# First attention, last two head pairs: the reciprocal of the denominators by exp(-ln) on ScalarE and a Newton step on VectorE

## The chip, the cores and the metric

The kernel runs on one core of one Trainium2 chip. The metric is the device time of one execution in microseconds (us), the median of the runs shown. A core has five engines that take their instructions in order and meet through semaphores: TensorE (PE, matrix products), VectorE (DVE), ScalarE (ACT, activations by function tables), GpSimd (POOL) and SyncE (SP, which issues most transfers here).

## The reference, cut to what matters

Two layers of a graph network with attention and feed-forward parts on 1250 tokens of width 1024. The change lies in the first layer's linear attention, 16 heads of 64 columns, which the kernel takes as 8 pairs of heads:

```
q = elu(xn @ Wq.T + bq) + 1
k = elu(xn @ Wk.T + bk) + 1
v = xn @ Wv.T + bv
KV = einsum('bhsd,bhsm->bhmd', k, v)
Z = 1 / (einsum('bhsd,bhd->bhs', q, k.sum(axis=2)) + 1e-06)
attn = einsum('bhsd,bhmd,bhs->bshm', q, KV, Z)
out = attn @ Wo.T + bo
```

Z is what the change computes in another way. The second layer's attention has no denominator.

## The kernel before, in words

Everything runs in single precision with each operand split into a high and a low part. The program is a row of phases: embedding, `attention` (tag m0), `project_and_count` (tag o), the graph layer (gl), routing and experts, and the same attention function again for layer two (tag m), its projection and the last feed-forward part. At the end of a phase all engines meet at a barrier (`Phase.__exit__`, L103), so the next phase begins when the slowest engine has arrived.

`attention` goes over j = 0 to 3, two head pairs at a time. A pair is called q here: 0 to 7, with A = 6 and B = 7 the last two. Tokens lie in three tiles t of 512, 496 and 242 columns. For each j TensorE computes keys and values in ten chunks (`keys`, L1632 to L1638), gathers the memory KV with the sum of the keys (`gather`, L1651), computes queries (`query`, L1613 to L1619) and then the numerator and the denominator of each tile (`attend`, L1668 to L1670), each in a PSUM bank of its own. `softly` is True in the first attention alone.

What follows `attend` is the stretch that the change touches. On ScalarE `den(q, t)` (L1751) waits for `at_done`, and for the `at_out` of the tile two before it, since `dn` has two slots; it copies the denominator plus 1e-6 into SBUF and raises `den_raw`. On VectorE `evict(q, t)` waits for `den_raw`, takes the reciprocal in place (L1869), drains, waits until the store of the pair before has left `ats`, multiplies it with the numerator (L1876) and raises `at_out`. SyncE then stores the tile (`store`, L1552), and TensorE may write the two banks again. The slots `dn` and `ats` lie in `xr`, of which 512 columns, 2560 to 3071, are unused.

The order on each engine is written out by hand. After the last keys it is, on ScalarE: `out_hi(0)`, `ask(B, 0)`, `memory`, `out_hi(1)`, `ask(B, 1)`, `out_hi(2)`, `out_hi(3)`, `den(A, 0)`, `ask_high(B, 0)`, `den(A, 1)`, `ask_high(B, 1)`, `ask(B, 2)`, `pairs_high`, `ask_high(B, 2)`, `one_high(A)`, `den(B, 0)`, `den(A, 2)`, `one_high(B)`, `den(B, 1)`, `den(B, 2)`. `ask` makes relu (L1732, L1733) and exp (L1736) of a query tile, `ask_high` (L1743) its high part, `out_hi` (L173) the high part of an output weight, `pairs_high` (L1780) that of the first token block of pairs 0 to 5, `one_high` (L1784) that of one more pair. On VectorE: `out_lo(0)`, `answer(B, 0)`, `memory` and `memory_low`, `out_lo(1)`, `answer(B, 1)`, `out_lo(2)`, `out_lo(3)`, `evict(A, 0)`, `ask_low(B, 0)`, `evict(A, 1)`, `ask_low(B, 1)`, `answer(B, 2)`, `pairs_low`, `ask_low(B, 2)`, `one_low(A)`, `evict(B, 0)`, `evict(A, 2)`, `one_low(B)`, `evict(B, 1)`, `evict(B, 2)`. On TensorE: `attend(A, 0)`, `attend(A, 1)`, `query(B, 2)`, `attend(A, 2)`, `attend(B, 0)`, `begin_out(0)`, `begin_out(1)`, `attend(B, 1)`, `begin_out(2)`, `begin_out(3)`, `attend(B, 2)`, and then 16 products that nobody reads (`fill`, L219), which follow `at_out[A, 2]`. `begin_out` (L365) is the first part of the next phase's product and waits for `pairs_low`.

ScalarE evaluates Exp, Ln, Sqrt, Tanh and Silu from tables. The loads of these tables (ACT_TABLE_LOAD) are no lines of the kernel's text: the compiler puts them into ScalarE's stream, and the trace gives each the line of the activation that it serves.

Of the kernel before, what the change touches and what calls it, by code (L numbers as in the profile page):

```python
# [10 lines left out]
ALU = mybir.AluOpType  # L11
ACT = mybir.ActivationFunctionType
AX = mybir.AxisListType

P = 128
N = 1250
E = 20000
D = 1024
# [204 lines left out]
def tile(t):  # L223
    return slice(CUTS[t], CUTS[t + 1])


def width(t):
    return CUTS[t + 1] - CUTS[t]


def flat(ap):
    return ap.rearrange("p a b -> p (a b)")
# [1234 lines left out]
def attention(nc, rest, tag, xh, xl, at, w_dram, bq_dram, bkv_dram, softly, raw, first, then, xr, xr_free, kept, ps, begun, place, onto, slots_free, freed, settled, beside=None, taken=(), room=None):  # L1467
# [5 lines left out]
    with Phase(nc, tag) as p:  # L1473
# [33 lines left out]
        qh, ql = p.sb("qh", [P, TM], F32R), p.sb("ql", [P, TM], F32R)  # L1507
        ks, mf = p.sb("ks", [P, 2]), own("mf", [P, 2, W2])
        mh, ml = p.sb("mh", [P, 2, W2], F32R), p.sb("ml", [P, 2, W2], F32R)
        spare = flat(xr)  # L1510
        ats, dn = spare[:, 0:TM], [spare[:, D + 512 * b:D + 512 * b + 512] for b in (1, 2)]
        bank = [ps[:, b] for b in range(8)]
        q_bank = lambda q, t: bank[3 - tile_nth[q, t] % 2][:, 0:width(t)]
# [12 lines left out]
        def num_den(q, t):  # L1526
            if t == 2:
                b = bank[0 if q % 2 == 0 else 1 if q == B else 7]
                return b[:, 0:width(t)], b[:, width(t):2 * width(t)]
            n, d = ((7, 6), (4 if softly else 6, 5))[t]  # L1530
            return bank[n][:, 0:width(t)], bank[d][:, 0:width(t)]
# [54 lines left out]
        @block.gpsimd  # L1586
        def _(e):
            e.wait_ge(*settled.last())
            for a in range(2):
                for b in range(2):  # L1590
                    i = e.memset(mask[64 * a:64 * a + 64, 64 * b:64 * b + 64], 1.0 if a == b else 0.0)
                i.then_inc(consts.sem)
                e.wait_ge(*consts["mask", a])
            for t in () if softly else xr_free[-1:]:
                e.wait_ge(*t.last())
            e.memset(mf[:], 0.0)
            e.memset(kv[:, 0, :, :, W2:KW].bitcast(F32), 1.0)
            e.memset(kv[:, 1, :, :, W2:KW].bitcast(F32), 0.0).then_inc(consts.sem)
            if beside:
                beside(e, p)  # L1600
# [113 lines left out]
        @block.scalar  # L1714
        def _(e):
            def hi(u):
                e.wait_ge(*arrived(u))
                if u[1] == Q:
                    e.wait_ge(*q_done[u[0] - 1, 2])
                elif u[0] >= 2:  # L1720
                    e.wait_ge(*kv_done[u[0] // 2 - 1, TC - 1])
                else:
                    e.wait_ge(*slots_free[kv_slot(u)])
                e.activation(held(0, u), raw[:, nth[u] % SLOTS], ACT.Copy).then_inc(high.sem)

            def ask(q, t):
                b, o, f, n = bq[:, q:q + 1], q_bank(q, t), qf[:, tile(t)], qn[:, tile(t)]
                e.wait_ge(*(q_done[q, t] if q or t else begun["q"]))
                if q:
                    e.wait_ge(*q_low[q - 1, t])  # L1730
                if softly:
                    e.activation(n, o, ACT.Relu, bias=nbq[:, q:q + 1], scale=-1.0)  # L1732
                e.activation(f, o, ACT.Relu, bias=b).then_inc(q_raw.sem)  # L1733
                e.drain()
                if softly:
                    e.activation(n, n, ACT.Exp, scale=-1.0).then_inc(q_exp.sem)  # L1736

            def ask_high(q, t):
                if softly:
                    e.wait_ge(*q_map[q, t])  # L1740
                if q:
                    e.wait_ge(*at_done[q - 1, t])
                e.activation(qh[:, tile(t)], qf[:, tile(t)], ACT.Copy).then_inc(q_high.sem)  # L1743

            def den(q, t):
                if softly:
                    n = out_nth[q, t]
                    e.wait_ge(*at_done[q, t])
                    if n >= 2:
                        e.wait_ge(*at_out[outs[n - 2]])  # L1750
                    e.activation(dn[n % 2][:, 0:width(t)], num_den(q, t)[1], ACT.Copy, bias=1e-6).then_inc(den_raw.sem)  # L1751

            def key(j, c):
                n, r = chunk_nth[j, c], rows_of(c)
                s = n % RING
                f = kvf[0:r, s].rearrange("p (q n) -> p q n", q=2)
                e.wait_ge(*kv_raw[j, c])
                if softly:
                    g = neg[0:r, s].rearrange("p (q n) -> p q n", q=2)
                    e.activation(g, f[:, :, 0:P], ACT.Relu, scale=-1.0)  # L1760
                    e.drain()
                    e.activation(g, g, ACT.Exp, scale=-1.0).then_inc(kv_exp.sem)
                    e.wait_ge(*kv_map[j, c])
                if n >= RING:
                    e.wait_ge(*m_used[chunks[n - RING]])
                e.activation(kv[0:r, 0, s, :, 0:W2], f, ACT.Copy).then_inc(kv_high.sem)  # L1766

            def memory(j):
                e.wait_ge(*m_raw[j])
                e.activation(mh[:, :, 0:MW], mf[:, :, 0:MW], ACT.Copy).then_inc(m_high.sem)  # L1770

            def out_hi(s):
                e.wait_ge(*ahead.loaded[s][s])
                e.wait_ge(*kv_done[J[-1], TC - 1])
                out.make_hi(e, s).then_inc(o_high.sem)

            def pairs_high():
                e.wait_ge(*pairs_in["pairs"])
                e.wait_ge(*q_done[B, 2])
                e.activation(oh[:, part], ar[:, part], ACT.Copy).then_inc(at_high.sem)  # L1780

            def one_high(q):
                e.wait_ge(*at_out[q, 0])
                e.activation(oh[:, q], ats[:, 0:P], ACT.Copy).then_inc(at_high.sem)  # L1784

            hi((0, K))
            hi((0, V))
            e.wait_ge(*ld["bq"])
            e.activation(nbq[:], bq[:], ACT.Copy, scale=-1.0)
            e.drain()  # L1790
            hi((1, K))
            hi((1, V))
            for t in xr_free if softly else ():
                e.wait_ge(*t.last())
            for j in J:
                a, b = 2 * j, 2 * j + 1
                if j == 0:
                    for t in T:
                        ask(a, t)
                    for t in T:  # L1800
                        ask_high(a, t)
                    hi((b, Q))
                else:
                    ask(a, 0)
                    hi((b, V))
                    den(a - 1, 0)
                    ask_high(a, 0)
                    ask(a, 1)
                    den(a - 1, 1)
                    ask_high(a, 1)  # L1810
                    hi((b, Q))
                    ask(a, 2)
                    den(a - 1, 2)
                    ask_high(a, 2)
                for c in C:
                    key(j, c)
                if j < J[-1]:
                    hi((a + 2, K))
                    ask(b, 0)
                    memory(j)  # L1820
                    hi((a + 2, V))
                    ask(b, 1)
                    hi((b + 2, K))
                    hi((a + 2, Q))
                    ask(b, 2)
                    for t in T:
                        den(a, t)
                        ask_high(b, t)
            out_hi(0)
            ask(B, 0)  # L1830
            memory(J[-1])
            out_hi(1)
            ask(B, 1)
            out_hi(2)
            out_hi(3)
            den(A, 0)
            ask_high(B, 0)
            den(A, 1)
            ask_high(B, 1)
            ask(B, 2)  # L1840
            pairs_high()
            ask_high(B, 2)
            one_high(A)
            den(B, 0)
            den(A, 2)
            one_high(B)
            den(B, 1)
            den(B, 2)

        @block.vector  # L1850
        def _(e):
# [12 lines left out]

            def evict(q, t):
                o, i = num_den(q, t)[0], dn[out_nth[q, t] % 2][:, 0:width(t)]
                if softly:
                    e.wait_ge(*den_raw[q, t])
                    e.reciprocal(i, i)  # L1869
                    e.drain()  # L1870
                else:
                    e.wait_ge(*at_done[q, t])
                if q:
                    e.wait_ge(*stored[t][q - 1])
                if softly:
                    e.tensor_tensor(ats[:, tile(t)], o, i, ALU.mult).then_inc(at_out.sem)  # L1876
                else:
                    e.tensor_copy(ats[:, tile(t)], o).then_inc(at_out.sem)
# [1535 lines left out]
```

## Time and profile before

| | us |
|---|---|
| median of 3 runs | 2318.83 |
| lowest, highest | 2316.47, 2319.75 |
| the profiled execution, its own time | 2314.61 |
| its span in the trace | 2312.9 |
| PE busy in it | 2226.0 (96%) |
| DVE busy | 1512.6 (65%) |
| ACT busy | 1015.3 (44%) |
| mean granted TensorE clock | 0.98 of full |

The span is the stretch from the first to the last instruction of the profiled execution; 1.7 us of its own time lie outside it. All start times in the rows are us from the span's start. "Busy" of an engine is the sum of its instructions' time; the granted clock is given as a share of full speed. The first attention runs from about 119 to 516.8 us of the span, and the last two pairs' `evict` from 490.9 to 514.3 us.

### The profile page before, as it was taken

Reading aid. Unit: us, or ns where it says so; the run is one execution under the profiler, and the core shown is the slowest. Engines: PE = TensorE matmul, PEld = TensorE weight load, DVE = VectorE, ACT = ScalarE, POOL = GpSimd, SP = SyncE. Lnnn points to the kernel's source line nnn. Section 1 sums busy time; section 2 is a strip of 40 time slices with the busy share of each in tenths; the row PEclk is TensorE's granted clock in tenths of the full one; section 3 lists DMA queues with packets and bytes.
Section 4 is the critical chain, followed back from the end, with each engine's and each line's share of the span. In section 5 each row is a group of like instructions: output and inputs, shape, how many; then the busy total and the mean of one; then the engine's idle time right before and its main releaser. Section 6 shows DMA issues by size and latency. Waiting matters only on the chain. (4 is left out here: it accounts for less than half of the span.)

```text
span 2312.9 us, 29634 instructions
## 1 busy us (share of the span) xinstructions
PE 2226.0 (96%) x10816; PEld 1820.2 (79%) x10816; DVE 1512.6 (65%) x2245; ACT 1015.3 (44%) x1515; POOL 253.9 (11%) x256
## 2 busy tenths in 40 slices
PE   7999999988989999989999999999999999999998
PEld 5788888867868888876888888867888888878886
DVE  8746374568869888866999999957743233345422
ACT  4134243338735545426888888851122122121220
POOL 0077773000010000030000000001000000000000
PEclk9999999999999999969999999999999999999999
DMA  5431231124448635164554555136421120134314
GB/s 191 160 99 41 50 79 29 62 73 142 146 170 318 238 133 220 63 255 141 192 199 177 208 178 188 65 103 214 135 86 35 48 82 31 59 106 153 121 46 150
DMA packets 114122, 299.91 MB, mean 130 GB/s; under 512 B 18802, under 2 KB 42218, under 8 KB 113974
## 3 DMA queue, kind: packets, MB, share of 16 engines
q1 hardware_dynamic: 103094, 276.52, 34.4%
q0 software_dynamic: 10880, 21.48, 3.3%
q8 instruction: 86, 1.41, 0.3%
q14 instruction: 62, 0.51, 0.1%
HBM read 295.24 MB, written 124.16 MB: 181 GB/s over the span
## 5 line engine op out<-in xcount | busy, mean ns | idle before, releaser
L2793 DVE TENSOR_TENSOR ex_wl<-exlast,ex_wh 128x1024 fp32r<-128x1024 f32 x216 | 252.9, 1220 | 9.1 <-ACT ex_wh L2862 8.6
L2862 ACT ACTIVATE ex_wh<-exlast 128x1024 fp32r<-128x1024 f32 x216 | 218.1, 1059 | 17.3 <-PE ex_pu L2816 8.5
L1322 POOL DMA_INDIRECT scratch_slots<-packed x160 | 197.4, 1234 | 57.4 <-issue 57.4
L365 PE MATMUL ps<-kept,xh 128*128 128x512 f32 (+2 forms) x480 | 159.2, 418 | 3.4 <-DVE xl L689 1.8
L1632 PE MATMUL ps<-kept,xl 128*128 128x512 f32 (+1 forms) x640 | 159.3, 391 | 0.0
L1634 PE MATMUL ps<-kept,xh 128*128 128x512 f32 (+1 forms) x640 | 158.4, 390 | 0.0
L1638 PE MATMUL ps<-kept,xh 128*128 128x512 f32 (+1 forms) x640 | 158.3, 390 | 0.0
L2192 PE MATMUL gl_bank<-gl_gh,gl_al 125*128 125x512 f32 x385 | 151.0, 392 | 3.1 <-DVE gl_al L2407 3.0
L2193 PE MATMUL gl_bank<-gl_gl,gl_ah 125*128 125x512 f32 x385 | 150.2, 390 | 0.0
L2194 PE MATMUL gl_bank<-gl_gh,gl_ah 125*128 125x512 f32 x385 | 150.0, 390 | 0.0
L1634 PEld LDWEIGHTS ps<-kept,xh 128*128 128x128 f32 (+1 forms) x640 | 118.6, 185 | 26.8
L1638 PEld LDWEIGHTS ps<-kept,xh 128*128 128x128 f32 (+1 forms) x640 | 118.6, 185 | 26.7
L2793 DVE TENSOR_TENSOR ex_wl<-exfirst,ex_wh 128x1024 fp32r<-128x1024 f32 x108 | 127.3, 1221 | 11.1 <-ACT ex_wh L2862 11.1
L1632 PEld LDWEIGHTS ps<-kept,xl 128*128 128x128 f32 (+1 forms) x640 | 114.4, 186 | 22.1
L2862 ACT ACTIVATE ex_wh<-exfirst 128x1024 fp32r<-128x1024 f32 x108 | 111.0, 1056 | 31.2 <-DMA exfirst<-in_experts 16.0
L1766 ACT ACTIVATE m_kv<-m_kvf 128x512 fp32r<-128x512 f32 (+1 forms) x40 | 25.3, 632 | 205.5 <-DVE m_kvf L1898 205.5
L1890 DVE TENSOR_TENSOR m_kvf<-ps,m_bkv 128x512 f32<-128x512 f32 (+1 forms) x40 | 27.7, 692 | 131.1 <-PE ps L1638 131.1
L365 PEld LDWEIGHTS ps<-kept,xh 128*128 128x128 f32 (+2 forms) x480 | 91.0, 190 | 25.6 <-DVE xl L689 2.0
L2250 ACT ACTIVATE gl_ah<-gl_thaf 125x625 fp32r<-125x625 f32 x80 | 58.2, 728 | 82.7 <-DVE gl_thaf L2397 82.7
L2816 PE MATMUL ex_pg<-ex_wl,ex_xh 128*128 128x512 f32 x216 | 89.4, 414 | 0.6 <-DVE ex_xl L2901 0.6
L2192 PEld LDWEIGHTS gl_bank<-gl_gh,gl_al 125*128 125x128 f32 x385 | 72.3, 188 | 20.3 <-DVE gl_al L2407 4.4
L2397 DVE TENSOR_TENSOR gl_thaf<-gl_thaf,counts 125x625 f32<-125x625 f32 x80 | 64.2, 807 | 33.0 <-ACT gl_thaf L2237 31.5
(530 smaller groups left out, 4968.8 us busy)
## 6 DMA issues: line engine op xcount, KB each, us to landing
exlast<-in_experts SPq DMA_DIRECT2D x216, 512.0 KB
exfirst<-in_experts SPq DMA_DIRECT2D x112, 512.0 KB
scratch_seats<-raw SPq DMA_DIRECT2D x95, 512.0 KB
raw<-in_qkv SPq DMA_DIRECT2D x48, 512.0 KB, 4.9
xr<-scratch_res SPq DMA_DIRECT2D x27, 512.0 KB, 4.1
xr<-scratch_seats SPq DMA_DIRECT2D x27, 512.0 KB
scratch_res<-xr SPq DMA_DIRECT2D x25, 512.0 KB, 3.6
raw<-in_wo SPq DMA_DIRECT2D x16, 512.0 KB, 5.4
```

The costliest lines, as they stand in the source:

```text
L365: i = e.matmul(o, a, b[:, cut], start=first and n == 0, stop=final and n == 2)
L1322: e.indirect_dma_start(dram["slot_rows"], bass.IndirectOffsetOnAxis(idx[:, k:k + 1].bitcast(U32), 0), pay[:, k, :], None).then_inc(scat.se ...
L1632: e.matmul(o, xl[:, k, tokens(c)], cut(wh, k), start=k == 0, stop=False)
L1634: e.matmul(o, xh[:, k, tokens(c)], cut(wh, k), start=False, stop=False)
L1638: m = e.matmul(o, xh[:, k, tokens(c)], cut(wl, k), start=False, stop=k == KC - 1)
L2192: e.matmul(o, al[0:r, b, d], gh[0:r, c], start=c == 0, stop=False)
L2193: e.matmul(o, ah[0:r, b, d], gl[0:r, c], start=False, stop=False)
L2194: m = e.matmul(o, ah[0:r, b, d], gh[0:r, c], start=False, stop=c == TC - 1)
L2397: e.tensor_tensor(af[0:r, (s + 2 * h) % 4, 0:HWID[h]], th[0:r, b, 0:HWID[h]], cnt[0:r, s, cols(h)], ALU.mult).then_inc(a_raw.sem)
L2793: return e.tensor_tensor(wl[:, n % RING], raw[unit[1]], wh[:, n % RING].bitcast(F32), ALU.subtract)
L2816: m = e.matmul(o[:], a[:, i % 2, k], w[:, n, cut], start=k == 0 and w is wl, stop=k == KC - 1 and a is xh and w is wh)
L2862: e.activation(wh[:, n % RING], raw[unit[1]], ACT.Copy).then_inc(high.sem)
```

## The change

Pairs 0 to 5 stay as they are. For pairs A and B, six tiles, `den` computes exp(-ln(d + 1e-6)) on ScalarE instead of a copy. `evict` takes that value i as a first approximation of the reciprocal, computes z = (d + 1e-6) * i, y = -o * i and (z - 2) * y on VectorE (one Newton step, with o the numerator), each a scalar_tensor_tensor with a drain between them. A column `eps` of 1e-6 is set by GpSimd for the bias of Ln, and one Ln of one column stands on ScalarE ahead of `out_hi(0)`. `z` lies in the unused part of `xr`.

```diff
@@ attention
+        eps = own("eps", [P, 2]) if softly else None
         spare = flat(xr)
+        near = spare[:, 2 * D + 512:3 * D]
@@ gpsimd
             e.memset(mf[:], 0.0)
+            if softly:
+                e.memset(eps[:], 1e-6)
@@ scalar, den
-                    e.activation(dn[n % 2][:, 0:width(t)], num_den(q, t)[1], ACT.Copy, bias=1e-6).then_inc(den_raw.sem)
+                    d, i = num_den(q, t)[1], dn[n % 2][:, 0:width(t)]
+                    if q < A:
+                        e.activation(i, d, ACT.Copy, bias=1e-6).then_inc(den_raw.sem)
+                    else:
+                        e.activation(i, d, ACT.Ln, bias=eps[:, 0:1])
+                        e.drain()
+                        e.activation(i, i, ACT.Exp, scale=-1.0).then_inc(den_raw.sem)
@@ scalar
+            if softly:
+                e.activation(eps[:, 1:2], eps[:, 0:1], ACT.Ln)
             out_hi(0)
             ask(B, 0)
@@ vector, evict
+                z, y = near[:, 0:width(t)], ats[:, tile(t)]
                 if softly:
                     e.wait_ge(*den_raw[q, t])
-                    e.reciprocal(i, i)
+                    if q < A:
+                        e.reciprocal(i, i)
+                    else:
+                        e.drain()
+                        e.scalar_tensor_tensor(z, num_den(q, t)[1], 1e-6, i, ALU.add, ALU.mult)
                     e.drain()
...
-                if softly:
+                if softly and q >= A:
+                    e.scalar_tensor_tensor(y, o, -1.0, i, ALU.mult, ALU.mult)
+                    e.drain()
+                    e.scalar_tensor_tensor(y, z, -2.0, y, ALU.add, ALU.mult).then_inc(at_out.sem)
+                elif softly:
                     e.tensor_tensor(ats[:, tile(t)], o, i, ALU.mult).then_inc(at_out.sem)
```

## Rows read from the trace of the kernel before

**Rows 1.** Busy time by stretch: us, PE, PEld, DVE, ACT, POOL, clock, DMA share, GB/s.

```profile
492.00:495.70 3.70, 0.03 (x1) 0.03 (x1) 3.63 (x4) 1.35 (x3) 0.00 (x0) 0.96 0.66 216
495.70:501.30 5.60, 2.90 (x6) 1.79 (x6) 5.53 (x6) 0.84 (x3) 0.00 (x0) 0.72 0.24 92
501.30:506.00 4.70, 4.66 (x13) 3.70 (x14) 4.53 (x5) 0.51 (x2) 0.00 (x0) 0.64 0.00 0
506.00:510.60 4.60, 4.60 (x24) 3.85 (x22) 4.52 (x5) 0.90 (x2) 0.00 (x0) 1.00 0.23 84
514.30:516.80 2.50, 0.00 (x0) 0.00 (x1) 0.00 (x0) 0.00 (x0) 0.00 (x0) 1.00 0.16 50
```

**Rows 2.** VectorE in order of time, end of the first attention: start, us, instruction.

```profile
490.89 3.35 DVE L1869 RECIPROCAL xr<-xr 128x512 f32<-128x512 f32 x1
494.31 0.69 DVE L1876 TENSOR_TENSOR xr<-ps,xr 128x512 f32<-128x512 f32 x1
...
500.34 0.95 DVE L1926 TENSOR_TENSOR ox<-ar,ox 128x768 fp32r<-128x768 f32 x1
...
512.11 1.66 DVE L1869 RECIPROCAL xr<-xr 128x242 f32<-128x242 f32 x1
513.84 0.41 DVE L1876 TENSOR_TENSOR xr<-ps,xr 128x242 f32<-128x242 f32 x1
```

**Rows 3.** TensorE in order of time, the same stretch; in brackets its idle time before.

```profile
501.34 4.61 PE L365 MATMUL ps<-kept,ox 128*128 128x512 f32 x12 [2.74 <-DVE ox L1926]
...
507.15 2.93 PE L365 MATMUL ps<-kept,ox 128*128 128x512 f32 x12
...
510.61 3.63 PE L219 MATMUL ps<-rest 128*128 128x512 bf16 x16
516.83 2.10 PE L219 MATMUL ps<-rest 128*128 128x512 bf16 x9 [2.59 <-PEq L103]
```

**Rows 4.** ScalarE in order of time, the same stretch.

```profile
480.28 0.68 ACT L1733 ACTIVATE counts<-ps,m_bq 128x512 f32<-128x512 f32 x1
481.04 0.63 ACT L1736 ACTIVATE counts<-counts 128x512 f32<-128x512 f32 x1
...
487.54 1.99 ACT L173 ACTIVATE kept<-raw 128x1024 fp32r<-128x1024 f32 x2
489.43 0.58 ACT L1751 ACTIVATE xr<-ps 128x512 f32<-128x512 f32 x1
...
500.45 0.41 ACT L1743 ACTIVATE m_qh<-counts 128x242 fp32r<-128x242 f32 x1 [7.02 <-DVE counts L1859]
...
506.06 0.31 ACT L1784 ACTIVATE ox<-xr 128x128 fp32r<-128x128 f32 x1 [4.25 <-DVE xr L1876]
```

**Rows 5.** ScalarE in order of time, the first Exp of this attention, with its table load.

```profile
128.26 0.68 ACT L1733 ACTIVATE counts<-ps,m_bq 128x512 f32<-128x512 f32 x1
129.00 1.28 ACT L1736 ACT_TABLE_LOAD   x1
130.30 0.63 ACT L1736 ACTIVATE counts<-counts 128x512 f32<-128x512 f32 x1
```

**Rows 6.** ScalarE's groups by line: table loads, count, busy, mean ns.

```profile
L302 ACT ACT_TABLE_LOAD x2 | 2.6, 1283 | 0.8 <-PEq L3406 0.8
L1736 ACT ACT_TABLE_LOAD x1 | 1.3, 1283 | 0.1
...
L3241 ACT ACT_TABLE_LOAD x1 | 1.3, 1283 | 0.0
```

**Rows 7.** Groups by line and shape, 200 to 515 us: busy, mean ns.

```profile
L1869 DVE RECIPROCAL xr<-xr 128x512 f32<-128x512 f32 x8 | 26.8, 3347 | 0.1
L1869 DVE RECIPROCAL xr<-xr 128x496 f32<-128x496 f32 x8 | 26.0, 3247 | 0.0
L1869 DVE RECIPROCAL xr<-xr 128x242 f32<-128x242 f32 x8 | 13.3, 1658 | 0.0
L1876 DVE TENSOR_TENSOR xr<-ps,xr 128x496 f32<-128x496 f32 x8 | 5.4, 675 | 0.6
L1894 DVE SCALAR_TENSOR_TENSOR counts<-counts 128x256 f32<-128x256 f32 x27 | 11.6, 430 | 26.2 <-ACT counts L1762 26.2
L1733 ACT ACTIVATE counts<-ps,m_bq 128x242 f32<-128x242 f32 x7 | 3.2, 454 | 0.0
```

**Rows 8.** GpSimd in order of time, start of the first attention.

```profile
120.19 0.11 POOL L1597 MEMSET m_kv<- 128x12 f32 x1
```

## The prediction

> **What bounds the kernel now.** I read the busy time by stretch first, then the engines in order of time in the last 25 us of the first attention, then the groups by shape for prices. The chain that ended last says nothing here, since it goes back only to the second half of the program. Before the wall VectorE has next to no gap: 5.53 of 5.60 us, 4.53 of 4.70, 4.52 of 4.60 [rows 1]. Its first reciprocal of these two pairs starts at 490.89 and its last instruction ends at 514.25 (513.84 + 0.41) [rows 2]. TensorE waits for it: 2.74 us for pairs_low (L1926), and its fill products end at 510.61 + 3.63 = 514.24 [rows 3]. So two engines reach the barrier together, and the next phase starts 2.6 us later, at 516.8 [rows 1, 3]. ScalarE has room: it waits 7.02 and 4.25 us for VectorE [rows 4]. What this stretch gains or loses passes whole into the time only if the later engine of the two moves, and ScalarE's room is finite.
>
> **What VectorE sheds.** Six reciprocals, two of each shape, go: 2 x (3.35 + 3.25 + 1.66) = 16.5 us [rows 7]. Each tile gets three scalar_tensor_tensor instead of one product. Of such an operation the rows have only 256 columns, 0.43 us; a two-operand product takes 0.69 for 512, 0.675 for 496 and 0.41 for 242 [rows 2, 7]. I take 0.69, 0.67 and 0.41; the low end is the product's price, the high end 2 x 0.43 = 0.86 for 512. After a drained instruction the next one starts 0.07 us later (490.89 + 3.35 = 494.24 against 494.31) [rows 2]. An evict of 512 goes from 3.35 + 0.07 + 0.69 = 4.11 to 3 x 0.69 + 2 x 0.07 = 2.21, one of 496 from 3.99 to 2.15, one of 242 from 2.14 to 1.37: 9.0 us less over six tiles, if i is ready in time.
>
> **What ScalarE takes on, without loads.** A Copy of 0.58 [rows 4] becomes Ln and Exp. Ln reads PSUM with a bias column as L1733 does, 0.68; Exp reads SBUF as L1736 does, 0.63; between them lie 0.08 (480.96 to 481.04) [rows 4]. That is 1.39 for 512, an estimated 1.36 for 496, and 0.454 + 0.08 + 0.41 = 0.94 for 242, with 0.41 from L1743, which reads SBUF too [rows 4, 7]. With 7.02 and 4.25 us of waiting [rows 4] this alone would be hidden.
>
> **The table loads.** Here the sum is decided. A switch of function costs a load of 1.28 us: it starts 0.06 after the activation before it has ended (128.94, 129.00), and the activation starts 0.02 after it (130.28, 130.30) [rows 5]. In drained order Exp starts at +1.36 instead of +0.08, so a load costs 1.28; in undrained order it also costs the overlap of about 0.1 that neighbours have, 1.4. The trace has nine loads: L302 twice, and one each at L1736, L2214, L2215, L2528, L2884, L3056 and L3241 [rows 6]. The tabled functions in order are Sqrt, Exp, Sqrt, Tanh, Sqrt, Exp, Silu, Sqrt, Silu: nine runs of one function and nine loads. No change of function came free, and none was served by a set fetched for an earlier function. No row shows Ln, so its load is bounded by zero (Ln and Exp under one load) and by one load at every change. I take every change, the pattern of all nine [rows 6]. Then the added single Ln loads one set, ask(B, 0)'s Exp the other, and each of the six dens loads twice: 14 loads, 18 us of ScalarE.
>
> [...]
>
> **The sum in order of time.** The single Ln and its load end before 477.6; out_hi(0) moves by 1.5, under VectorE's wait for answer(B, 0) and without price. The load ahead of ask(B, 0)'s Exp moves answer(B, 0), memory and what follows on ScalarE by 1.28: out_hi(3) ends at 490.8 instead of 489.5 (487.54 + 1.99) [rows 4]. From there, starts overlapped as now:
> den(A, 0) takes 1.28 + 0.02 + 0.68 + 0.06 + 1.28 + 0.02 + 0.63 = 3.97 and ends at 494.8. VectorE, free at about 492.3 (out_lo(3) is late by 1.3 too), waits 2.5; evict(A, 0) ends at 497.05 instead of 495.0 (494.31 + 0.69) [rows 2].
> ask_high(B, 0), then den(A, 1) of 3.9, end at 499.3; evict(A, 1) ends at 501.5, and ask_low(B, 1), answer(B, 2) and pairs_low follow until 503.2, where they now end at 501.29 (500.34 + 0.95) [rows 2]: 1.9 later. TensorE's begin_out and all behind it move by 1.9, its fill ends at 516.2.
> ScalarE gets answer(B, 2) at 502.4, does ask_high(B, 2) and one_high(A) until 503.0, den(B, 0) until 507.0, den(A, 2) of 3.5 until 510.5, one_high(B), den(B, 1) until 514.7, den(B, 2) until 518.25. Nothing but these loads holds it now: the waits for at_done are over before each. VectorE's evict(B, 2) of 1.37 ends at 519.65 instead of 514.25.
> That is **+5.4 us** at the barrier, with ScalarE as the new bound. The 16.5 us of reciprocals are all given back as VectorE's waits for den_raw. The low end: one load fewer in the chain, +4. The high end: three operations at 0.86 on the last tiles, and a colder TensorE after the wall (below), +8.
>
> **The rest.** GpSimd's memset of two columns is like L1597, 0.11 us [rows 8], 11 us ahead of the first Exp at 130.30 [rows 5] and before its queue of scatters, which it moves by that 0.1 at most: nothing. No transfer is added. The six stores follow at_out, so the last ones go out 5.4 later; the projection reads them behind the barrier that moves with them. The waits of SyncE have nothing else queued behind them. The z slot is unused space. The drain ahead of z comes after a wait, on an empty engine. TensorE's pause at the wall grows from 2.59 [rows 3] to about 6 us (516.2 to 522.2). The clock was granted at 0.72 and 0.64 after pauses of 3.7 and 2.74 us, where twelve products of 512 took 4.61 instead of 2.93 us [rows 1, 3]. [...]
>
> **Own time and median.** The sum is made against the profiled execution, 2314.61 us, span 2312.9. That is 4.2 us (0.18%) under the median of 2318.83. The difference is set on the median: 2318.83 + 5.4 = 2324.2. What a measurement of this kernel can tell from no change is about 0.2%, 4.6 us; the forecast lies just beyond it.
>
> **Rival 1: one set serves both (not slower).** Ln and Exp stay under one table load, that of the added single Ln, which falls into slack. Then den(A, 0) ends at 489.43 + 1.39 = 490.8, as VectorE comes free at 490.9; evict(A, 0) ends 1.85 earlier, evict(A, 1) 3.7, and pairs_low at 497.6 instead of 501.3. TensorE's row of begin_out, attend, begin_out, attend and fill follows without a gap and ends at 514.24 - 3.65 = 510.6, VectorE at 509.4. So TensorE's fill sets the wall and the gain is 3.65 us, not 9: 2315.2, or 2313.5 if the shorter pauses keep the clock up and begin_out takes 2.93 instead of 4.61 [rows 1, 3]. It decides if no load stands in den. For it: the single Ln is placed where only a set that serves both would make sense of it. Against: the nine loads at nine changes [rows 6].
> [...] No row shows Ln under any load. Chance 0.13.
>
> **Rival 2: a load costs more in the pipeline.** If a load between two activations also empties the pipe for over a microsecond, as no row shows but the drained order might bring, all 13 loads in the chain grow: at 1 us each 13 us more, +18, 2337. Against it: 0.06 and 0.02 [rows 5]. Chance 0.04.
>
> **Rival 3: the loads come, but less of them counts.** Some lie in waits that I took as over, such as den(B, 1)'s and den(B, 2)'s for TensorE, or VectorE's operations are dearer while ScalarE is late anyway and hide. The wall then moves by under 4.6 us, most likely +3: 2321.8. It is the lower part of my forecast's own spread. Chance 0.25, against 0.58 for the forecast proper.
>
> **How the numbers follow.** Forecast and rivals 2 and 3 give slower or slightly slower. The range has to hold the forecast's +4 to +8, rival 3 and the scatter of medians (2316.5 to 2319.8 for one kernel); it leaves out most of rivals 1 and 2: 2317.5 to 2329.5. Faster by over 0.2%: rival 1 with the clock held, 0.05. Slower by over 0.2%: the forecast and rival 2, 0.62. Within: rival 3 and the rest of rival 1, 0.33.
>
> **What would show it.** Right: 23 table loads instead of 9, two in each den; no reciprocal after 490; VectorE waiting for ACT at L1751's successor before each z, about 2 us at a time; the fill ending about 3 us before VectorE; the next phase starting near 522. Wrong: one or two more loads only (rival 1: TensorE's fill last, next phase near 513); a gap of about a microsecond beside each load (rival 2); loads with ScalarE waiting between them (rival 3); scalar_tensor_tensor of 512 far from 0.69 us.

## The result and the profile after

The change makes the kernel slightly slower: 2322.57 us median of 11 runs (2319.52 to 2325.31) against 2318.76 of 11 runs before (2316.47 to 2320.0), ratio 1.0016, 95% interval 1.0009 to 1.0024, so 3.8 us (2.1 to 5.6). That lies in the stated range and in the forecast's direction, but inside the 0.2% that the prediction called no change.

First ScalarE's groups by line, table loads only. The six single loads in the phases behind are there as before [rows 6], so there are 23 loads instead of 9.

```profile
L1759 ACT ACT_TABLE_LOAD x6 | 7.7, 1283 | 0.1
L1761 ACT ACT_TABLE_LOAD x6 | 7.7, 1283 | 0.3
L302 ACT ACT_TABLE_LOAD x2 | 2.6, 1283 | 0.8 <-PEq L3429 0.8
L1740 ACT ACT_TABLE_LOAD x2 | 2.6, 1283 | 0.1
L1840 ACT ACT_TABLE_LOAD x1 | 1.3, 1283 | 0.0
```

L1759 is Ln in den, L1761 its Exp, L1840 the single Ln, L1740 the Exp in ask. Each den loads twice, and the Exp of ask(B, 0), which had its table, loads again behind the single Ln. ScalarE in order of time, the last pairs of the changed kernel (beside [rows 4, 5] of before):

```profile
476.94 0.63 ACT L1776 ACTIVATE m_kv<-counts 98x512 fp32r<-98x512 f32 x1 [0.49 <-DVE counts L1917]
477.59 1.28 ACT L1840 ACT_TABLE_LOAD   x1
...
481.25 0.69 ACT L1736 ACTIVATE counts<-ps,m_nbq 128x512 f32<-128x512 f32 x1 [1.21 <-PE ps L1623]
...
482.58 1.28 ACT L1740 ACT_TABLE_LOAD   x1
...
490.37 2.00 ACT L173 ACTIVATE kept<-raw 128x1024 fp32r<-128x1024 f32 x2
492.39 1.28 ACT L1759 ACT_TABLE_LOAD   x1
493.68 0.69 ACT L1759 ACTIVATE xr<-ps,counts 128x512 f32<-128x512 f32 x1
494.43 1.28 ACT L1761 ACT_TABLE_LOAD   x1
495.72 0.63 ACT L1761 ACTIVATE xr<-xr 128x512 f32<-128x512 f32 x1
...
504.04 0.41 ACT L1747 ACTIVATE m_qh<-counts 128x242 fp32r<-128x242 f32 x1 [0.79 <-DVE counts L1871]
...
518.13 1.28 ACT L1761 ACT_TABLE_LOAD   x1
519.42 0.41 ACT L1761 ACTIVATE xr<-xr 128x242 f32<-128x242 f32 x1
```

From 492.39 to 519.83 ScalarE has one wait, 0.79 us. Its two longest waits before were 7.02 and 4.25 us [rows 4]. VectorE in order of time, first and last evict (beside [rows 2]):

```profile
496.45 0.69 DVE L1886 SCALAR_TENSOR_TENSOR xr<-ps,xr 128x512 f32<-128x512 f32 x1 [2.64 <-ACT xr L1761]
497.22 0.69 DVE L1895 SCALAR_TENSOR_TENSOR xr<-ps,xr 128x512 f32<-128x512 f32 x1
497.98 0.69 DVE L1897 SCALAR_TENSOR_TENSOR xr<-xr 128x512 f32<-128x512 f32 x1
...
503.92 0.95 DVE L1949 TENSOR_TENSOR ox<-ar,ox 128x768 fp32r<-128x768 f32 x1
...
519.93 0.41 DVE L1886 SCALAR_TENSOR_TENSOR xr<-ps,xr 128x242 f32<-128x242 f32 x1 [1.35 <-ACT xr L1761]
...
520.90 0.41 DVE L1897 SCALAR_TENSOR_TENSOR xr<-xr 128x242 f32<-128x242 f32 x1
```

VectorE now waits for ScalarE's Exp before each of the six evicts, 1.30 to 3.32 us at a time, 12.8 us in all. TensorE in order of time (beside [rows 3]):

```profile
504.93 5.49 PE L365 MATMUL ps<-kept,ox 128*128 128x512 f32 x12 [2.65 <-DVE ox L1949]
...
515.27 3.63 PE L219 MATMUL ps<-rest 128*128 128x512 bf16 x16
523.98 4.00 PE L219 MATMUL ps<-rest 128*128 128x512 bf16 x9 [5.08 <-PEq L103]
```

TensorE's fill ends at 518.90, 2.4 us before VectorE at 521.31. So ScalarE's chain, through VectorE, alone sets the barrier.

To compare profiles I use **the stretch**: from the start of the last high part of keys and values (m_kv, the first line of ScalarE above) to the first transfer issued in the projection. All profiles, in us; "ahead" runs to the first relu of the attention, "pairs 0 to 5" from there to the stretch, "projection" from the stretch's end to the first table load of the graph layer, "rest" to the end of the span. begin_out is the first group of 12 products in the stretch.

| kernel | added loads | ahead | pairs 0 to 5 | stretch | begin_out | projection | rest |
|---|---|---|---|---|---|---|---|
| before | 0 | 127.7 | 347.7 | 41.41 | 4.61 | 158.0 | 1638.1 |
| before2 | 0 | 130.7 | 347.8 | 41.40 | 4.33 | 159.1 | 1638.8 |
| changed | 14 | 129.3 | 347.6 | 47.01 | 5.49 | 158.8 | 1638.2 |
| again | 14 | 129.3 | 347.7 | 47.00 | 5.36 | 158.4 | 1638.8 |
| fill26 | 14 | 130.6 | 347.6 | 46.99 | 5.29 | 158.0 | 1639.9 |
| recip_kept | 14 | 129.6 | 347.7 | 50.75 | 4.60 | 158.9 | 1637.6 |
| nowarm | 12 | 130.8 | 347.7 | 45.71 | 5.49 | 158.8 | 1642.2 |
| paired | 10 | 129.5 | 347.7 | 45.30 | 5.08 | 158.3 | 1638.4 |
| oneset | 1 | 129.2 | 347.7 | 36.04 | 3.06 | 158.2 | 1638.1 |
| oneset2 | 1 | 128.7 | 347.9 | 36.00 | 3.03 | 158.2 | 1639.3 |
| oneset_fill8 | 1 | 130.3 | 347.6 | 36.86 | 4.41 | 158.0 | 1636.1 |
| oneset_all | 0 | 131.2 | 344.7 | 37.60 | 4.21 | 158.6 | 1638.5 |
| copied | 0 | 129.3 | 347.6 | 36.00 | 3.03 | 158.2 | 1640.8 |

Ratios below are against runs of the kernel before taken beside the others: medians 2320.38 us for again, oneset, copied and nowarm, 2317.51 for fill26, recip_kept, oneset_fill8 and oneset_all, 2316.75 for paired. Outside oneset_all, which changes more than the stretch, the difference of two such medians comes out between 3.1 us under and 0.8 us over what the stretch shows. So the medians give the direction, and the stretch the size.

### The profile page after: what moved, and what is told of

The parts are those of the page before. It is cut to its first block and busy times, and to the rows that moved or that the text cites. A ratio compares the mean times of both kernels' runs of the same rounds, so it can differ in the third digit from the quotient of the medians.

```text
span 2320.9 us, 29680 instructions
## 1 busy us (share of the span) xinstructions
PE 2233.4 (96%) x10816; PEld 1825.3 (79%) x10816; DVE 1503.5 (65%) x2251; ACT 1037.4 (45%) x1536; POOL 253.1 (11%) x257
## 5 line engine op out<-in xcount | busy, mean ns | idle before, releaser
L1638 PE MATMUL ps<-kept,xh 128*128 128x512 f32 (+1 forms) x640 | 158.3, 389 | 0.0
L1642 PE MATMUL ps<-kept,xh 128*128 128x512 f32 (+1 forms) x640 | 158.2, 389 | 0.0
```

The lines of the kernel that those rows point to most:

```text
L1638: e.matmul(o, xh[:, k, tokens(c)], cut(wh, k), start=False, stop=False)
L1642: m = e.matmul(o, xh[:, k, tokens(c)], cut(wl, k), start=False, stop=k == KC - 1)
```

## The experiments

**again** and **before2**, both kernels unedited.

> The changed kernel once more, unedited. 'The stretch' is here and below the time from the start of the last high part of keys and values in the first attention (98 rows, ScalarE) to the first transfer issued in the projection; it is 516.79 - 475.38 = 41.4 us before and 523.95 - 476.94 = 47.0 us after. If the 5.6 us are the change's, this profile has 46.9 to 47.1 again and the time is 3.8 to 5.6 us above before's. If they were scatter of one execution, the stretch comes out elsewhere between 41 and 47.

> The kernel before, unedited, for a second profile. Theory (what lies outside the stretch is scatter): the stretch is 41.4 us again, and the part ahead of it, which reached the last high part of keys and values at 475.4 us in the first profile and at 476.9 to 478.4 in those of the changed kernels, comes out within 475 to 479. Rival (the change costs 1.5 us ahead of the stretch): 475.4 again.

again: 2322.93 us, ratio 1.0016 (1.0007 to 1.0025), stretch 47.00. The medians differ by 2.6 us, or 3.7 by the ratio, just under the 3.8 to 5.6 expected. before2, a single run: 2319.46 us, stretch 41.40. ScalarE and SyncE in before2, the two lines that bound its stretch, and between them the last instructions of TensorE and VectorE:

```profile
478.51 0.63 ACT L1766 ACTIVATE m_kv<-counts 98x512 fp32r<-98x512 f32 x1 [0.49 <-DVE counts L1894]
...
513.43 3.63 PE L219 MATMUL ps<-rest 128*128 128x512 bf16 x16
...
516.96 0.41 DVE L1876 TENSOR_TENSOR xr<-ps,xr 128x242 f32<-128x242 f32 x1
...
519.91 0.32 SPq L1094 DMA_DIRECT2D o_slots<-scratch_slots  x1
```

The stretch repeats within 0.01 us in either kernel, so the 5.6 us are the change's. What lies ahead varies by 3 us between two profiles of one and the same kernel, and the changed kernel's later arrival lies within that. Here TensorE's fill ended at 517.06, 0.31 us before VectorE at 517.37, and the stretch was the same: it is VectorE, 2.54 us ahead of the next phase in both profiles of before, that sets the barrier there.

**oneset**: a table set, number 6 in the edit, is loaded by hand ahead of the single Ln; that it serves both Ln and Exp is shown by this run's rows.

```diff
             if softly:
+                e.add_instruction(mybir.InstLoadActFuncSet(name=nc.get_next_instruction_name(), act_func_set_id=6))
                 e.activation(eps[:, 1:2], eps[:, 0:1], ACT.Ln)
```

> One edit to the changed kernel: the table set that holds both Ln and Exp is loaded by hand ahead of the single Ln, so that no further load is needed in the attention (1 added load instead of 14). Theory (ScalarE's loads are the bound): VectorE's evicts start as ScalarE's Exp ends, TensorE's fill becomes last, and the stretch is 41.4 - 3.65 = 37.8 us; the time is 3.7 us below before's, 7 to 9 below the changed kernel's. Rival (VectorE's three operations with drains, or the clock, cost what the change lost): the stretch stays above 43 us.

2312.01 us, ratio 0.997 (0.996 to 0.998), stretch 36.04. That is 11 us off the changed kernel's stretch and 5.4 off before's. The trace has 10 table loads instead of 23: the nine of before and the one by hand (L1840), of 1.28 us. None stands in a den or ahead of ask(B, 0)'s Exp (L1740): in each den Exp starts 0.06 to 0.07 us after Ln has ended (491.62, 491.68), with no load between them. ScalarE, then TensorE, then VectorE of oneset in order of time:

```profile
477.54 1.28 ACT L1840 ACT_TABLE_LOAD   x1
478.83 0.20 ACT L1841 ACTIVATE counts<-counts 128x1 f32<-128x1 f32 x1
...
482.55 0.63 ACT L1740 ACTIVATE counts<-counts 128x512 f32<-128x512 f32 x1
...
490.95 0.67 ACT L1759 ACTIVATE xr<-ps,counts 128x512 f32<-128x512 f32 x1
491.68 0.63 ACT L1761 ACTIVATE xr<-xr 128x512 f32<-128x512 f32 x1
...
503.95 0.67 ACT L1759 ACTIVATE xr<-ps,counts 128x496 f32<-128x496 f32 x1 [0.78 <-PE ps L1674]
```

```profile
495.51 0.47 PE L1672 MATMUL ps<-m_ql,m_mh 128*128 128x512 f32 x1 [1.94 <-DVE m_ql L1876]
...
499.51 3.06 PE L365 MATMUL ps<-kept,ox 128*128 128x512 f32 x12 [2.37 <-DVE ox L1950]
...
507.17 3.63 PE L219 MATMUL ps<-rest 128*128 128x512 bf16 x16
```

```profile
492.58 0.69 DVE L1887 SCALAR_TENSOR_TENSOR xr<-ps,xr 128x512 f32<-128x512 f32 x1
...
509.37 0.41 DVE L1898 SCALAR_TENSOR_TENSOR xr<-xr 128x242 f32<-128x242 f32 x1
```

Exp needs no load there, ScalarE waits for TensorE again (0.78 us), VectorE ends at 509.78 and TensorE's fill at 510.80: the fill is last, as rival 1 had it. The expected 37.8 took begin_out at 4.61; it took 3.06, which is nearly all of the difference of 1.8 (the parts are in the account of rival 1 below). With and without 13 of the loads, the same Ln, Exp and three operations differ by 11 us, so the rival that blames VectorE's operations falls.

**copied**: it leaves out Ln and Exp, the single Ln too, so its output is not the attention's.

```diff
-                        e.activation(i, d, ACT.Ln, bias=eps[:, 0:1])
-                        e.drain()
-                        e.activation(i, i, ACT.Exp, scale=-1.0).then_inc(den_raw.sem)
+                        e.activation(i, d, ACT.Copy, bias=1e-6, scale=1e-9).then_inc(den_raw.sem)
```

> Leaves out Ln and Exp: for the last two pairs ScalarE makes one scaled copy, as long as the copy before; VectorE does the three operations of the Newton step on it. Theory: no loads, ScalarE has room again, so the stretch is as with the one set, 37.8 us or up to 0.7 less (Ln and Exp gone from between TensorE's last product and evict), bounded by TensorE's fill. Rival (VectorE's chain bounds it once the loads are gone): the stretch is over 0.5 us shorter than with the one set, and VectorE's last instruction ends after the fill.

2315.57 us, ratio 0.998 (0.9971 to 0.9989), stretch 36.00, the same as with the one set to 0.04 us. Ln and Exp themselves cost nothing on the path; the loads do. VectorE ends at 509.18, the fill at 510.76. Its median lies 3.6 us above oneset's at the same stretch; the part called rest has 2.7 us of that in the profiles, and why stays open.

**nowarm**: the line `e.activation(eps[:, 1:2], eps[:, 0:1], ACT.Ln)` is taken out.

> One edit to the changed kernel: the single Ln ahead of out_hi(0) is left out, so its load and the load ahead of ask(B, 0)'s Exp go (12 added loads instead of 14). Theory (loads count one for one where ScalarE has no slack behind them): the load ahead of the single Ln was hidden, the one at ask(B, 0) was not, so the stretch is 1.3 us shorter, 45.7. Rival (loads this early are hidden anyway): 47.0 as before the edit.

2323.51 us, ratio 1.0015 (1.0005 to 1.0025), stretch 45.71, 1.3 less, the value expected for one load on the path and one in slack. The load of the single Ln is the one in slack: behind it, in the changed kernel, ScalarE still waits 1.21 us for TensorE before ask(B, 0). The medians cannot tell 1.3 us; the stretch can.

**paired**: the first four dens in two groups.

```diff
-            den(A, 0)
+            dens((A, 0), (A, 1))
             ask_high(B, 0)
-            den(A, 1)
             ask_high(B, 1)
...
-            den(B, 0)
-            den(A, 2)
+            dens((B, 0), (A, 2))
```

with `dens` doing Ln of both, one drain, Exp of both.

> The changed kernel with its dens in two groups: Ln of (A, 0) and (A, 1), then Exp of both; Ln of (B, 0) and (A, 2), then Exp of both. No set is chosen by hand; 10 added loads instead of 14. Theory (ScalarE's stream, loads included, is the bound until its waits for others come back): evict(A, 1) starts 1.1 us earlier, pairs_low and begin_out too, den(B, 1) then waits for TensorE's attend(B, 1), and the stretch is 45.4 us (45.0 to 45.9), not 47.0. Rival (loads count one for one): 47.0 - 4 x 1.3 = 41.8.

2321.43 us, ratio 1.0019 (1.0009 to 1.0029), stretch 45.30, 1.7 less for four loads. ScalarE of paired in order of time:

```profile
503.30 0.41 ACT L1747 ACTIVATE m_qh<-counts 128x242 fp32r<-128x242 f32 x1 [2.68 <-DVE counts L1882]
...
503.92 1.28 ACT L1770 ACT_TABLE_LOAD   x1
505.22 1.04 ACT L1770 ACTIVATE xr<-ps,counts 128x512 f32<-128x512 f32 x2
506.31 1.28 ACT L1774 ACT_TABLE_LOAD   x1
507.61 0.92 ACT L1774 ACTIVATE xr<-xr 128x512 f32<-128x512 f32 x2
510.60 0.31 ACT L1807 ACTIVATE ox<-xr 128x128 fp32r<-128x128 f32 x1 [2.07 <-DVE xr L1908]
```

With fewer loads it waits again, 2.68 us instead of 0.79 for answer(B, 2) and 2.07 for evict(B, 0), so loads do not count one for one once the waits return. The size is as expected, but the second wait is for VectorE, not for TensorE's attend(B, 1).

**recip_kept**: the exp/ln part alone, with `ACT.Exp` of +ln and VectorE's old reciprocal and product for pairs A and B.

> The changed kernel without the Newton step: Ln and Exp with all their loads stay on ScalarE, with exp(+ln), and VectorE takes the reciprocal of it and one product, as before the change. Theory (ScalarE's loads bound the stretch, VectorE's saving lies in their shade): the stretch grows by much less than the 9.0 us that VectorE has more to do. evict(A, 1) and so answer(B, 2), for which ScalarE waits, come 2.1 to 3.7 us later, and the last evict takes 2.1 instead of 1.4: 49.5 to 51.4 us. Rival (VectorE's operations bound it): 47 + 9 = 56.

2325.08 us, ratio 1.0031 (1.0018 to 1.0043), stretch 50.75. VectorE has 9.0 us more to do than in the changed kernel (the prediction's sum) and the stretch grows by 3.7. VectorE, then ScalarE:

```profile
496.70 3.35 DVE L1882 RECIPROCAL xr<-xr 128x512 f32<-128x512 f32 x1 [2.56 <-ACT xr L1761]
500.12 0.69 DVE L1895 TENSOR_TENSOR xr<-ps,xr 128x512 f32<-128x512 f32 x1
```

```profile
506.26 0.41 ACT L1747 ACTIVATE m_qh<-counts 128x242 fp32r<-128x242 f32 x1 [2.70 <-DVE counts L1871]
```

So the two halves of the change stand apart. Ln and Exp with their loads cost 9.3 us (41.41 to 50.75), and on that chain the Newton step is worth 3.7 (50.75 to 47.0). Without loads it is worth 5.4 (41.4 to 36.0, copied).

**fill26**: `fill(e, bank[0], rest, 26 if softly else 6)`.

> One edit to the changed kernel: 26 products in TensorE's fill instead of 16, which nobody reads. They end at 515.3 + 26 x 0.227 = 521.2, as VectorE's last evict does (521.3), so the stretch stays 47.0. Theory (the long pause at the barrier lets TensorE's clock drop, which costs at the start of the projection): the pause is 2.6 to 2.8 instead of 5.1 us, the nine products after it take 2.1 instead of 4.0 us, and the projection, from its first transfer to the graph layer's first table load, is 158.0 to 158.2 us as before, not 158.4 to 158.9. Rival (the projection waits for weights anyway and its length is scatter): the nine products are faster and the projection is not shorter.

2323.08 us, ratio 1.0023 (1.0014 to 1.0032), stretch 46.99. TensorE in order of time:

```profile
516.09 5.79 PE L219 MATMUL ps<-rest 128*128 128x512 bf16 x26
525.22 3.53 PE L219 MATMUL ps<-rest 128*128 128x512 bf16 x9 [3.35 <-PEq L103]
```

The stretch is as expected. The rest is a miss: the pause was 3.35, not 2.6 to 2.8, the nine products were still slow, and yet the projection took 158.0 us, as short as in the first profile of before, where they took 2.10. before2 has 3.05 us for the nine and 159.1. So no run gives a price for the colder start: the projection's 158.0 to 159.1 us follow neither the pause nor the nine products.

**oneset_fill8** and **oneset2**: the kernel with one set, with 8 fill products, and once more as it is.

> The kernel with one table set, and 8 instead of 16 products in TensorE's fill. Theory (with the loads gone TensorE's fill is last, 510.8 against VectorE's 509.8): the barrier comes 1.0 us earlier, the stretch is 35.0 instead of 36.0, and VectorE's evict(B, 2) is last. Rival (something else, such as SyncE's last store, holds the barrier): 36.0 again. The time is within scatter of the kernel with one set.

> The kernel with one table set once more, for a second profile. Up to TensorE's fill it is the same program as the one with 8 fill products, whose begin_out took 4.41 us against 3.06 here, and whose stretch was 36.9 against 36.0. Theory (the clock during begin_out differs from one execution to the next, at the same pause of 1.95 us): begin_out takes 2.9 to 4.6 us, the stretch is 36.0 to 37.6, and the two go together. Rival (the fill's length sets the clock or the stretch): 3.06 and 36.0 again.

oneset_fill8: 2310.05 us, ratio 0.9969 (0.9958 to 0.9981), stretch 36.86, longer where 35.0 was expected. oneset2, a single run: 2311.67 us, stretch 36.00. TensorE and VectorE of oneset_fill8:

```profile
496.56 0.61 PE L1672 MATMUL ps<-m_ql,m_mh 128*128 128x512 f32 x1 [1.95 <-DVE m_ql L1876]
...
500.56 4.41 PE L365 MATMUL ps<-kept,ox 128*128 128x512 f32 x12 [1.25 <-DVE ox L1950]
...
509.56 1.90 PE L219 MATMUL ps<-rest 128*128 128x512 bf16 x8
```

```profile
511.76 0.41 DVE L1898 SCALAR_TENSOR_TENSOR xr<-xr 128x242 f32<-128x242 f32 x1
```

Busy time by stretch of oneset_fill8, then of oneset, us, PE, PEld, DVE, ACT, POOL, granted clock, DMA share, GB/s:

```profile
499.00:502.50 3.50, 2.25 (x6) 1.56 (x6) 2.81 (x7) 2.57 (x6) 0.00 (x0) 0.50 0.19 73
```

```profile
499.00:502.50 3.50, 2.99 (x13) 2.45 (x14) 2.73 (x6) 2.19 (x6) 0.00 (x0) 1.00 0.05 20
```

Two things. The fill, ending at 511.46, is no longer last: VectorE ends at 512.17 and the projection starts 2.64 us after it. In oneset it starts 2.13 after the fill and 3.15 after VectorE. And begin_out took 4.41 here, 3.06 and 3.03 in oneset and oneset2. The pause before attend(B, 0) was the same, 1.94 to 1.95 us, but here the lower clock was already there in attend(B, 0) (0.53 in the mean over it against 1.00 in oneset; its first product took 0.61 us against 0.47) and lasted into begin_out: 0.50 against 1.00 from 499.0 to 502.5. The fill starts 31.61 us into the stretch instead of 30.28. Taking that 1.33 off gives 36.86 - 1.33 = 35.5, an estimate: the shorter fill would be worth 0.5 us, not 1.0, since the next phase follows VectorE by 2.64 us and TensorE by 2.13. oneset2 came out at the very values that its rival named (3.03 and 36.00), which the theory's range holds too, so it does not decide whether the fill's length or chance set the clock. Against the rival stands oneset_all below: 16 fill products, the same pause of 1.95 us, and a begin_out of 4.21.

**oneset_all**: the set is loaded after the query biases, the single Ln is out, and all eight pairs use Ln, Exp and the Newton step.

> The set that holds Ln and Exp is loaded at the start of the first attention, and all eight pairs use Ln, Exp and the Newton step. Theory (the stretch of the last pairs is the only one where VectorE is on the path; pairs 0 to 5 lie beside TensorE's keys and queries): the stretch is 36.0 as with one set for two pairs, and the 348 us from the first Exp to the stretch shorten only by TensorE's waits for evict, 0 to 2 us; the time is 7 to 9 us below before's. Rival (VectorE's reciprocals hold pairs 0 to 5 too): over 3 us more is gained there.

2309.59 us, ratio 0.9961 (0.9949 to 0.9974), the lowest ratio of all, though its interval overlaps oneset's. Pairs 0 to 5 take 344.7 instead of 347.7, but 1.3 of that is the first Exp's load, which now stands ahead of the first relu. ScalarE of oneset_all, the first Exp and the start of the stretch:

```profile
132.51 0.63 ACT L1740 ACTIVATE counts<-counts 128x512 f32<-128x512 f32 x1
...
475.90 0.63 ACT L1776 ACTIVATE m_kv<-counts 98x512 fp32r<-98x512 f32 x1 [0.49 <-DVE counts L1917]
```

From the first Exp to the stretch, as the expectation has it, are 343.4 us, against 475.38 - 130.30 = 345.1 before [rows 5]: 1.7 less, within the 0 to 2 expected. So nearly all of the 18 other reciprocals lay beside TensorE's work. The stretch is 37.60, not 36.0, since begin_out took 4.21: attend(B, 0) still ran fast here (1.00) and the clock fell in begin_out (0.68 in the mean over it).

## Why the prediction was right

**The loads.** The step that decided was taken as it came: one load at every change of function, 14 added, 23 in all. The trace shows that the load fetched for the single Ln did not serve Exp, and oneset shows that a set serving both exists and needs one load of 1.28 us. Rival 1 (chance 0.13) was thus a true account of another program, not of this one. The nine loads of before could not decide it, since no row shows two functions under one load; that the pattern holds for Ln and Exp too is what the changed kernel's trace adds. Nor was a set serving both fetched by itself where Ln and Exp alternate, as rival 1 had it: the six dens have 12 loads in the changed kernel's trace, and none once set 6 is asked for.

**The sum.** Against the stretch's start, with the changed kernel's times less 1.56 (476.94 - 475.38): den(B, 2) ends at 518.27 (forecast 518.25), pairs_low at 503.3 (503.2), the last evict at 519.75 (519.65). The next phase starts 2.64 us after VectorE instead of 2.54, and with this 0.1 the stretch grows by 5.6, where 5.4 was forecast. A scalar_tensor_tensor of 512 took 0.69, as taken. The upper end of the spread, +8, counts a colder TensorE after the wall. No run shows that price: the nine products after the wall took 4.00 us at a granted clock of 0.51 instead of 2.10 at 1.00, and the projection 158.8 us, where the two profiles of before have 158.0 and 159.1. TensorE's fill ended 1.1 later than forecast, most of it since begin_out took 5.49 instead of 4.61; it had slack. Two readings of the prediction are off and change nothing. The 16.5 us of reciprocals cannot all be given back as waits, as the three operations take 7.5 us more than the product did: the waits were 12.8 us, and VectorE came to them 1.3 late. And the memset of [rows 8] lies 10 us ahead of the first Exp, not 11.

**A load's price.** Activations start 0.01 to 0.02 after each load and loads 0.02 to 0.06 after the activation ahead, in drained order too. A drained Exp behind a load began 2.0 us after Ln's own start (493.68, 495.72), which is Ln's 0.69, the load's 1.28 and 0.07 of gaps. Rival 2 falls.

**Rival 3** had loads that lie in waits. There was one wait of 0.79 us in the chain, so none of the dens' loads was hidden. The smaller figure of the median, 3.8 where the stretch has 5.6, is not its doing.

**Stretch and median.** 5.6 us is the upper edge of the interval (2.1 to 5.6) and within again's 1.6 to 5.8. Outside the stretch no part of the changed kernel's profiles moved by more than the unedited kernels do between themselves. Whether 1 to 2 us come back somewhere stays open: the parts ahead and behind scatter by 3 us and more, and the median of before itself was 2318.76, 2320.38, 2317.51 and 2316.75 in four sets of runs. The forecast laid 0.62 on more than 0.2% and 0.33 on less; the measured 0.16% is the latter.

**Rival 1's size.** Its 3.65 us kept begin_out at 4.61; the gain was 5.4, close to the 5.3 that it named for a fast begin_out, but not by its sum. In oneset begin_out starts 3.3 us earlier in the stretch than before (3.7 forecast), TensorE's work up to the fill is 1.6 shorter by the clock (1.00 in begin_out against 0.64 [rows 1]), and the next phase starts 2.13 us after TensorE where it started 2.54 after VectorE, 0.4 less. The prediction took both engines as equal at the barrier, 514.24 and 514.25; by these gaps (an estimate) TensorE had 0.4 us to spare. That term was left out.

## What to carry to other kernels

Here Ln alternating with Exp cost a table load of 1.28 us at each change, since the set fetched for the one did not serve the other. Count such loads in the trace, and see whether one set, loaded by hand, serves both: here set 6 did, and that turned a loss of 5.6 us in the stretch into a gain of 5.4. Work moved from a full engine to one with room must fit that room in its place in the order: ScalarE's two longest waits made 11 us; Ln and Exp fitted in, 13 loads of 1.28 did not. Where the change is near what medians can tell, a stretch between two fixed instructions settles what medians leave open: it repeated within 0.01 us in either kernel, and within 0.04 in oneset. But where TensorE is last it holds TensorE's clock as well, worth 1.3 to 1.6 us in oneset_fill8 and oneset_all.

## What was not expected

The same pause of 1.94 to 1.95 us before attend(B, 0) led to three courses of the clock. It stayed at 1.00 in oneset, oneset2 and copied (begin_out 3.06, 3.03 and 3.03 us). It was down in attend(B, 0) already (0.53) and 0.50 at the start of begin_out in oneset_fill8 (4.41). It fell only in begin_out in oneset_all (1.00 over attend(B, 0), 0.68 over begin_out, 4.21 us). This was worth 1.3 to 1.6 us of the stretch, and no run here shows what decides it.

The next phase starts 2.13 to 2.14 us after TensorE's last instruction where TensorE is last. Where VectorE is last it starts 2.64 us after VectorE's, in all the kernels with loads in den and in oneset_fill8, and 2.54 after it in the two profiles of before.

Nine fill products after the barrier took 2.1 to 4.0 us with no trace of it in the projection's length.
